# Masking the local attention on VectorE instead of by matmul, in an eight-stage transformer on one Trainium2 core

## The chip, the cores and the metric

The program runs on one core of a Trainium2 chip. The metric is the time of one launch in device microseconds. Before the change it is 4281.75 us, the median of 3 runs (4274.94 to 4282.47).

## What is computed

The reference chains eight stages over x of shape (2, 1024, 256). The change lies in one of them, the stage of `_L2_ffn_setup`: six layers, each a local attention followed by a gated feed-forward part.

```python
def attn_layer(x, Wqkv, qs, ksc, Wo):          # 16 heads of 64
    q, k, v = split(x @ Wqkv)
    q, k = l2norm(q) * qs, l2norm(k) * ksc     # l2norm: t / max(norm(t), 1e-12)
    q, k = rotary(q), rotary(k)
    # windows of 64 rows; each looks at the window before it and at itself: 128 keys
    sim = einsum(q, [k before, k own]) * 8
    sim = where(key later than the row, or over 64 before it, or absent, -max, sim)
    return softmax(sim) @ [v before, v own] -> @ Wo

def ffn_layer(x, g, bln, W1, b1, W2, b2):      # inner width 682
    a, gate = split((layernorm(x) * g + bln) @ W1 + b1)
    return (a * gelu(gate)) @ W2 + b2
```

Both are residual: each is added to x. A token shift precedes the projections.

## The kernel before

All work is written out by hand: each engine has its own list of instructions, in the order in which it executes them, and the engines meet by semaphores. A layer is two blocks, one for attention and one for the feed-forward part; at the end of a block the engines wait for each other.

**Attention** (lines 1660 to 1985). The 2048 tokens are 16 tiles of 128 rows, and each tile has two halves of 8 heads, so a layer has 32 halves, u = 2n + i. The engines work on different halves at once:

- TensorE (PE), for each u: `turn_ready(u)` (L1715, transposes of q and k), `project(n+1, i, 0)` and `project(n+1, i, 1)` (L1705: q and k of the half two ahead), `scores(u)` (L1742, L1747), `turn_probs(u-1)` (L1715), `project(n+1, i, 2)` (v), `attend(u-1)` (L1764). In the last tile `attention_out` (L1776), 16 matmul records, stands in the place of the projections. A projection writes PSUM bank 0 or 1 in turn, and waits until the bank's last contents are read: part 0 for `rotate` of the half before, part 1 for ScalarE's copy `value` of the half before, part 2 for `rotate` of part 0.
- ScalarE (ACT), for each u: `turned_query` (L1831), `turned_key` (L1838, L1839), `value` (L1859), `norms` (L1822, L1824), `square` twice (L1814), `turned_probs(u-1)` twice (L1845), `exp(u)` (L1849), `out(u-1)` (L1864). ACT does them in this order; `out(u-1)` and all that follows stand behind `exp(u)`.
- VectorE (DVE), for each u: `rotate(n+1, i, 0)` (L1907, L1909), `shift(u)` (L1925 maximum, L1929 subtraction), `rotate(n+1, i, 1)`, `row_sums(u)` (L1936, L1938), `sums(n+1, i)` (L1917 twice, and the guard L1920, which takes the maximum with 1e-24).
- GpSimd (POOL), for each u: `scale_probs(u-1)` twice (L1985), `scale` twice (L1978, waits for `norms`), `pair` twice (L1972, each waits for its `rotate`).
- SyncE issues the copies of v into the next window's place (L1684, L1688).

The mask is a bf16 tile of 0 and -1e30, and `scores` first multiplies an identity by it into the PSUM bank (four matmuls of 64x64 by 512, L1742) and then adds the scores of q and k to it (16 matmuls, L1747). A fp32 matmul leaves two records in the trace. The next half's scores may start when `shift` has read the bank.

**Feed-forward part** (lines 2000 to 2250). It goes over four groups g of 512 tokens: `up` (L2090, L2095), GELU on ACT, `gated` on DVE (L2208), `down` (L2108), `add_ffn` on DVE (L2222). The inner width 682 makes five chunks of 128 rows and a rest of 42. `down(g)` goes for each of the two output halves c through the six chunks, the rest last, into PSUM bank c. TensorE's order ends with up(2), down(1), up(3), down(2), down(3).

## Time and profile before

| | |
|---|---|
| median of 3 runs | 4281.75 us (4274.94 to 4282.47) |
| the profiled execution | 4293.74 us, its span 4291.9 us |
| busy, share of the span | PE 91%, PEld (weight loads) 49%, DVE 58%, ACT 46%, POOL 38% |
| granted TensorE clock, mean | 0.958 |
| local transformer, six layers | from about 860 to 3877 us of the span; attention some 334 us of a layer, feed-forward some 169 |
| DMA | 43 GB/s mean over the span |

A row of a timeline has the start in us from the span's start, the time it took in us, the engine, the line of the kernel, the operation, the tile written <- tiles read, shapes, and how many instructions the row merges. In brackets behind it stands how long the engine was idle before it, and what it was waiting for.

### The profile page before, as it was taken

Reading aid. Unit: us, or ns where it says so; the run is one execution under the profiler, and the core shown is the slowest. Engines: PE = TensorE matmul, PEld = TensorE weight load, DVE = VectorE, ACT = ScalarE, POOL = GpSimd, SP = SyncE. Lnnn points to the kernel's source line nnn. Section 1 sums busy time; section 2 is a strip of 40 time slices with the busy share of each in tenths; the row PEclk is TensorE's granted clock in tenths of the full one; section 3 lists DMA queues with packets and bytes.
Section 4 is the critical chain, followed back from the end, with each engine's and each line's share of the span. In section 5 each row is a group of like instructions: output and inputs, shape, how many; then the busy total and the mean of one; then the engine's idle time right before and its main releaser. Section 6 shows DMA issues by size and latency. Waiting matters only on the chain. (4 is left out here: it accounts for less than half of the span.)

```text
span 4291.9 us, 68832 instructions
## 1 busy us (share of the span) xinstructions
PE 3893.8 (91%) x26876; PEld 2084.4 (49%) x26887; DVE 2490.1 (58%) x3426; ACT 1953.7 (46%) x3526; POOL 1637.2 (38%) x1428
## 2 busy tenths in 40 slices
PE   6769976899999999999999999999999999998755
PEld 4434333555544555445544555445554455545522
DVE  4564555578823886258842788238862588424533
ACT  3555443556622664336632566326643366323411
POOL 0520321066611664036630566116641366300044
PEclk9989987999999999999999999999999999998877
DMA  4010000111110111001110111101110011100296
GB/s 147 1 39 3 0 0 10 57 44 30 26 61 16 29 29 58 20 24 29 30 67 0 34 28 27 61 15 29 29 52 26 24 28 30 48 0 11 90 287 188
DMA packets 95344, 185.48 MB, mean 43 GB/s; under 512 B 14004, under 2 KB 46256, under 8 KB 94000
## 3 DMA queue, kind: packets, MB, share of 16 engines
q1 hardware_dynamic: 86816, 169.02, 13.2%
q0 software_dynamic: 6144, 9.44, 1.2%
q8 instruction: 217, 3.56, 0.4%
q10 hardware_dynamic: 2064, 2.62, 0.2%
q14 instruction: 103, 0.84, 0.1%
HBM read 112.19 MB, written 20.09 MB: 31 GB/s over the span
## 5 line engine op out<-in xcount | busy, mean ns | idle before, releaser
L1705 PE MATMUL PS<-locw,X 128*128 128x512 f32 x2304 | 1066.3, 599 | 28.9 <-PEq L133 13.1
L1972 POOL TENSOR_TENSOR locm<-locm 128x512 f32<-128x512 f32 x384 | 489.1, 1274 | 921.1 <-DVE locm L1909 920.8
L1705 PEld LDWEIGHTS PS<-locw,X 128*128 128x128 f32 x2304 | 394.9, 190 | 441.6 <-issue 309.8
L2090 PE MATMUL PS<-locxn,locw 128*128 128x512 f32 x960 | 435.9, 612 | 19.8 <-DVE loch L2208 19.8
L1978 POOL TENSOR_TENSOR locm<-locm,locrn 128x512 f32<-128x512 f32 x384 | 392.4, 1043 | 128.6 <-ACT locrn L1824 128.6
L1985 POOL TENSOR_TENSOR locpr<-locpr,locrs 128x512 f32<-128x512 f32 x384 | 391.0, 1039 | 128.8 <-DVE locrs L1938 109.0
L1907 DVE TENSOR_TENSOR locm<-PS,loctab 128x512 f32<-128x512 f32 x384 | 263.3, 686 | 211.8 <-ACT locsq L1814 211.8
L1845 ACT ACTIVATE locpt<-PS 128x512 f32<-128x512 f32 x384 | 208.4, 594 | 322.2 <-PE PS L1715 322.2
L2208 DVE SCALAR_TENSOR_TENSOR loch<-PS,locvec,locgl 128x512 f32<-128x512 f32 x144 | 106.8, 748 | 370.4 <-PE PS L2090 280.9
L2090 PEld LDWEIGHTS PS<-locxn,locw 128*128 128x128 f32 x960 | 185.9, 196 | 267.0 <-issue 237.2
L1849 ACT ACTIVATE locpr<-locpr 128x1024 f32<-128x1024 f32 x192 | 203.4, 1060 | 190.9 <-DVE locpr L1929 190.9
L1925 DVE TENSOR_REDUCE locnm<-PS 128x8 f32<-128x1024 f32 x192 | 234.8, 1223 | 87.0 <-PE PS L1747 81.9
L2108 PE MATMUL PS<-loch,locw 128*128 128x512 f32 (+1 forms) x576 | 265.4, 606 | 0.0
L1909 DVE TENSOR_TENSOR locm<-PS,loctab 128x512 f32<-128x512 f32 x384 | 261.1, 680 | 0.0
L1814 ACT ACTIVATE locsq<-PS 128x512 f32<-128x512 f32 x384 | 223.6, 589 | 42.9 <-PE PS L1705 27.9
L1929 DVE TENSOR_TENSOR locpr<-PS,locnm 128x1024 f32<-128x1024 f32 x192 | 235.1, 1224 | 6.6
L1936 DVE TENSOR_REDUCE locrs<-locpr 128x8 f32<-128x1024 f32 x192 | 234.2, 1220 | 6.7 <-ACT locpr L1849 6.7
L1917 DVE TENSOR_REDUCE locss<-locsq 128x8 f32<-128x512 f32 x384 | 238.0, 662 | 0.0
L2160 ACT ACTIVATE locgl<-PS,locvec 128x512 f32<-128x512 f32 x120 | 81.1, 686 | 343.3 <-PE PS L2090 343.1
L1764 PEld LDWEIGHTS PS<-locpt,locve 128*64 128x64 f32 x3072 | 154.9, 137 | 149.5 <-issue 132.0
L2069 PE MATMUL PS<-BIG,locwo 128*128 128x512 f32 x480 | 211.1, 597 | 5.7 <-PEq L1675 5.7
L1764 PE MATMUL PS<-locpt,locve 128*64 128x64 f32 x3072 | 198.8, 228 | 13.3 <-ACT locpt L1845 13.3
(326 smaller groups left out, 6363.4 us busy)
## 6 DMA issues: line engine op xcount, KB each, us to landing
locve<-locva SPq DMA_DIRECT2D x372, 128.0 KB, 2.2
locw<-in_L2f_wqkv SPq DMA_DIRECT2D x36, 512.0 KB, 9.9
BIG<-in_L3f_gu SPq DMA_DIRECT2D x16, 768.0 KB, 10.1
moe_sums<-none SPq DMA_DIRECT2D x2, 4352.0 KB, 24.0
locw<-in_L2f_w SPq DMA_DIRECT2D x6, 1386.0 KB
BIG<-moe_sums SPq DMA_DIRECT2D x16, 512.0 KB, 10.5
moewp<-in_L3f_gu SPq DMA_DIRECT2D x10, 768.0 KB, 14.4
loctab<-in_L2f_tabs SPq DMA_DIRECT2D x6, 1024.0 KB, 12.2
```

Of the source, the lines that this page charges most:

```text
L1705: mm = pe.matmul(PS[:, o % 2, :], k.X[:, j, at - j:at - j + P], W[:, j, col:col + G], start=j == 0, stop=j == KD - 1)
L1764: mm = pe.matmul(PS[r * HD:(r + 1) * HD, 6 + u % 2, t * P + w * WIN:t * P + (w + 1) * WIN], v[:, 8 * i + 2 * t + r, :], PT[:, 2 * (u % 2) ...
L1907: dve.tensor_tensor(heads(M1[:, j, :]), raw, tab[0], ALU.mult)
L1909: dve.tensor_tensor(M2[:, x, :].rearrange("p (h u d) -> p h u d", h=8, u=2), halves, tab[1].rearrange("p h (u d) -> p h u d", u=2), ALU.mu ...
L1917: op = dve.tensor_reduce(SS[:, i, m, :], heads(SQ[:, m, :]), AX.X, ALU.add)
L1925: dve.tensor_reduce(NM[:, u % 2, :], view, AX.X, ALU.max, negate=True).then_inc(s.negmax, 1)
L1929: dve.tensor_tensor(PR[:, u % 2, :, :], view, NM[:, u % 2, :].unsqueeze(2).to_broadcast([P, 8, P]), ALU.add).then_inc(s.shifted, 1)
L1972: pool.tensor_tensor(M1[:, j, :], M1[:, j, :], M2[:, x, :], ALU.add).then_inc(s.paired, 1)
L1978: pool.tensor_tensor(heads(M1[:, j, :]), heads(M1[:, j, :]), RN[:, i, x, :].unsqueeze(2).to_broadcast([P, 8, HD]), ALU.mult).then_inc(s.re ...
L1985: pool.tensor_tensor(pr, pr, RS[:, u % 2, 4 * x:4 * x + 4].unsqueeze(2).to_broadcast([P, 4, P]), ALU.mult).then_inc(s.probs, 1)
L2090: mm = pe.matmul(PS[:, 4 + 2 * (m % 2) + half, :], W1[:, c, at:at + P], XNL[:, g % 2, c, :], start=c == 0, stop=c == KD - 1)
L2108: mm = pe.matmul(PS[:, c, :], W2[0:r, m, c * P:(c + 1) * P], H[0:r, g % 2, m, :], start=m == 0, stop=m == FM - 1)
```

## The change

The mask no longer goes through TensorE. Its tile is fp32, 128 by 2 by 128 (a quarter of the size), and DVE adds it when it copies the scores from PSUM into the tile PR of the probabilities; the maximum and the subtraction then read PR. TensorE's wait before the next scores is for that first copy (`masked`). The rest is smaller: the guard of the sums takes its constant from a tile TINY by `tensor_tensor` instead of as an immediate by `tensor_scalar`; the squares of the two halves have buffers of their own, and ACT does the first square of a half ahead of `norms`; in `down` the rests of both output halves are laid on rows 0 to 41 and 64 to 105, with a second copy of the rest's weights (one more DMA) and of its activations (one more DVE copy for each group), and are multiplied after the ten full chunks; `down` alternates between banks 0, 1 and 2, 3.

```diff
-    mask = np.stack([np.tile(np.concatenate([v, own], 1), (1, 4)) for v in (none, before)], 1).astype(f)
+    earlier = [np.where(np.arange(P)[:, None] < WIN, none, before), before]
+    mask = np.stack([np.concatenate([v, own], 1) for v in earlier], 1).astype(f)
...
         def make_first(pool):
-            pool.wait_ge(s.mask_loaded, 16)
-            pool.tensor_copy(MASKB[:, :, :], MASKF)
             make_tables(pool, 0)
...
-                SQ = sa(f"locsq_{layer}", [P, 2, G])
+                SQ = sa(f"locsq_{layer}", [P, 2, 2, G])
...
                                 if u:
-                                    pe.wait_ge(s.shifted, HALVES * layer + u)
+                                    pe.wait_ge(s.masked, HALVES * layer + u)
...
                         def scores(u):
-                            for r in range(2):
-                                for w in range(2):
-                                    kind = 0 if n % NT == 0 and w == 0 else 1
-                                    pe.matmul(PS[w * WIN:(w + 1) * WIN, 4 + r, :], k.identb[...], MASKB[...], start=True, stop=False)
                             for t in range(4):
...
-                                                       start=False, stop=t == 3)
+                                                       start=True, stop=True)
...
                         def square(n, i, x):
-                            if n or i:
-                                act.wait_ge(s.sums_guarded, HALVES * layer + 2 * n + i)
-                            act.activation(SQ[:, x, :], PS[:, (3 * i + x) % 2, :], ACT.Square).then_inc(s.squared, 1)
+                            if n:
+                                act.wait_ge(s.sums_guarded, HALVES * layer + 2 * (n - 1) + i + 1)
+                            act.activation(SQ[:, i, x, :], PS[:, (3 * i + x) % 2, :], ACT.Square).then_inc(s.squared, 1)
...
                                 value((u - 1) // 2 + 1, (u - 1) % 2)
+                            if more:
+                                square(n + 1, i, 0)
+                            if u and (u - 1) // 2 < TILES - 1:
                                 norms((u - 1) // 2 + 1, (u - 1) % 2)
                             if more:
-                                square(n + 1, i, 0)
                                 square(n + 1, i, 1)
...
-                            dve.tensor_scalar(SS[:, i, :, :], SS[:, i, :, :], 1e-24, None, ALU.max).then_inc(s.sums_guarded, 1)
+                            dve.tensor_tensor(SS[:, i, :, :], SS[:, i, :, :], TINY[:, :, :], ALU.max).then_inc(s.sums_guarded, 1)
...
                         def shift(u):
-                            dve.wait_ge(s.scores, HALVES * layer + u + 1)
-                            dve.tensor_reduce(NM[:, u % 2, :], view, AX.X, ALU.max, negate=True).then_inc(s.negmax, 1)
-                            dve.wait_ge(s.negmax, HALVES * layer + u + 1)
                             if u >= 2:
                                 dve.wait_ge(s.turned_in_psum, probs_turn(u - 2, 1) + 1)
-                            dve.tensor_tensor(PR[:, u % 2, :, :], view, NM[:, u % 2, :].unsqueeze(2).to_broadcast([P, 8, P]),
+                            dve.wait_ge(s.scores, HALVES * layer + u + 1)
+                            dve.tensor_tensor(pr, view, MASK[:, kind, :].unsqueeze(1).to_broadcast([P, 8, P]),
+                                              ALU.add).then_inc(s.masked, 1)
+                            dve.wait_ge(s.masked, HALVES * layer + u + 1)
+                            dve.tensor_reduce(NM[:, u % 2, :], pr, AX.X, ALU.max, negate=True).then_inc(s.negmax, 1)
+                            dve.wait_ge(s.negmax, HALVES * layer + u + 1)
+                            dve.tensor_tensor(pr, pr, NM[:, u % 2, :].unsqueeze(2).to_broadcast([P, 8, P]),
                                               ALU.add).then_inc(s.shifted, 1)
...
                         def down(g):
                             pe.wait_ge(s.h, FM * (n0 + g) + FM + 2)
+                            pe.wait_ge(s.rest, n0 + g + 1)
+                            at = 2 * (g % 2)
                             for c in range(KD):
...
-                                for m in range(FM):
-                                    r = rows(m)
-                                    mm = pe.matmul(PS[:, c, :], W2[0:r, m, c * P:(c + 1) * P], H[0:r, g % 2, m, :],
-                                                   start=m == 0, stop=m == FM - 1)
-                                mm.then_inc(s.y_in_psum, 1)
+                                for m in range(FM - 1):
+                                    pe.matmul(PS[:, at + c, :], W2[0:FR, m, c * P:(c + 1) * P], H[0:FR, g % 2, m, :],
+                                              start=m == 0, stop=False)
+                            for c in range(KD):
+                                r = slice(c * GATE_AT, c * GATE_AT + last)
+                                pe.matmul(PS[:, at + c, :], W2[r, FM - 1, c * P:(c + 1) * P], H[r, g % 2, FM - 1, :],
+                                          start=False, stop=True).then_inc(s.y_in_psum, 1)
...
                         def gated(g):
...
+                            dve.wait_ge(s.h, FM * (n0 + g) + FM + 2)
+                            dve.tensor_copy(H[GATE_AT:GATE_AT + last, g % 2, FM - 1, :], H[0:last, g % 2, FM - 1, :]).then_inc(s.rest, 1)
```

## Rows read from the trace of the kernel before

**Rows 1.** Windows: busy us of PE, PEld, DVE, ACT, POOL, then clock; attention, feed-forward.

```profile
900.00:1000.00 100.00, 100.00 (x1006) 58.91 (x1005) 87.49 (x118) 63.00 (x127) 70.00 (x65) 1.00 0.13 30
1200.00:1340.00 140.00, 135.74 (x310) 57.84 (x306) 32.73 (x47) 40.67 (x54) 13.88 (x9) 0.98 0.13 46
```

**Rows 2.** Timeline of ACT: exp of one half, out and value behind it.

```profile
1011.88 1.06 ACT L1849 ACTIVATE locpr<-locpr 128x1024 f32<-128x1024 f32 x1 [0.89 <-DVE locpr L1929]
1013.15 0.60 ACT L1864 ACTIVATE BIG<-PS 128x512 f32<-128x512 f32 x1 [0.21 <-PE PS L1764]
...
1014.96 0.62 ACT L1859 ACTIVATE locva<-PS 128x512 f32<-128x512 f32 x1
```

**Rows 3.** Timeline of PE and PEld around two halves' scores.

```profile
1008.00 0.41 PE L1742 MATMUL PS<-locmaskb,identb 64*64 64x512 bf16 x4
1008.24 1.04 PE L1747 MATMUL PS<-lockt,locqt 64*64 64x128 f32 x32
...
1013.96 3.65 PE L1705 MATMUL PS<-locw,X 128*128 128x512 f32 x8
...
1015.63 0.30 PEld L1705 LDWEIGHTS PS<-locw,X 128*128 128x128 f32 x2 [0.61 <-ACT locva L1859]
```

**Rows 4.** Source L1859, who waited for it; source L1864, until when idle (us, times).

```profile
  PEld PS L1705: 106.5, 174
...
  PE PS L1764: 40.9, 160
```

**Rows 5.** Timeline of DVE in the same half.

```profile
1009.36 1.22 DVE L1925 TENSOR_REDUCE locnm<-PS 128x8 f32<-128x1024 f32 x1
1010.62 1.22 DVE L1929 TENSOR_TENSOR locpr<-PS,locnm 128x1024 f32<-128x1024 f32 x1
...
1015.61 0.96 DVE L1920 TENSOR_SCALAR locss<-locss 128x16 f32<-128x16 f32 x1
1017.58 0.69 DVE L1907 TENSOR_TENSOR locm<-PS,loctab 128x512 f32<-128x512 f32 x1 [1.01 <-ACT locsq L1814]
```

**Rows 6.** Timeline of POOL in the same half.

```profile
1009.66 1.27 POOL L1972 TENSOR_TENSOR locm<-locm 128x512 f32<-128x512 f32 x1
...
1014.50 2.04 POOL L1985 TENSOR_TENSOR locpr<-locpr,locrs 128x512 f32<-128x512 f32 x2
1017.21 1.04 POOL L1978 TENSOR_TENSOR locm<-locm,locrn 128x512 f32<-128x512 f32 x1 [0.67 <-ACT locrn L1824]
```

**Rows 7.** Sources: DVE operations by line, shortest/median/longest ns, first and last start.

```profile
L1929 DVE TENSOR_TENSOR locpr<-PS,locnm x192: 1223/1224/1226, 887.0 to 3696.7; 128x1024 f32<-128x1024 f32 x192
L1936 DVE TENSOR_REDUCE locrs<-locpr x192: 1219/1220/1222, 889.4 to 3699.0; 128x8 f32<-128x1024 f32 x192
L2559 DVE TENSOR_TENSOR moeroom<-moeroom,moets x1: 1225/1225/1225, 4072.2 to 4072.2; 128x1024 f32<-128x1024 f32 x1
L185 DVE TENSOR_TENSOR X<-lnxc,lnrs x8: 676/678/1607, 852.3 to 857.4; 128x512 f32<-128x512 f32 x8
L1920 DVE TENSOR_SCALAR locss<-locss x192: 174/957/959, 875.4 to 3676.7; 128x16 f32<-128x16 f32 x192
```

**Rows 8.** Timeline of ACT: exp of halves 0 and 29 of the first layer.

```profile
888.28 1.06 ACT L1849 ACTIVATE locpr<-locpr 128x1024 f32<-128x1024 f32 x1 [3.17 <-DVE locpr L1929]
...
1164.72 1.06 ACT L1849 ACTIVATE locpr<-locpr 128x1024 f32<-128x1024 f32 x1 [0.88 <-DVE locpr L1929]
```

**Rows 9.** Timelines of PE and DVE at the end of the first layer's feed-forward part.

```profile
1328.36 17.43 PE L2090 MATMUL PS<-locxn,locw 128*128 128x512 f32 x40
1345.63 1.88 PE L2095 MATMUL PS<-locxn,locw 128*106 128x512 f32 x4
...
1363.97 0.75 DVE L2222 SCALAR_TENSOR_TENSOR X<-PS,locvec,X 128x512 f32<-128x512 f32 x1 [4.79 <-PE PS L2108]
1369.51 0.75 DVE L2222 SCALAR_TENSOR_TENSOR X<-PS,locvec,X 128x512 f32<-128x512 f32 x1 [4.79 <-PE PS L2108]
```

**Rows 10.** Timeline of POOL: the tables made before the first layer.

```profile
861.77 4.49 POOL L1614 TENSOR_TENSOR loctab<-loctab,locrows 128x2048 f32<-128x2048 f32 x1 [8.41 <-DMA locrows<-in_L2f_rows]
```

More of the change, by code:

```diff
@@ L1568, in stage_local_transformer @@
     (
-        s.mask_loaded, s.weights, s.tables, s.tables_made, s.layer_vectors, s.wo_loaded, s.ffn_loaded, s.cleared,
+        s.mask_loaded, s.tiny, s.weights, s.tables, s.tables_made, s.layer_vectors, s.wo_loaded, s.ffn_loaded, s.cleared,
         s.projected, s.squared, s.rotated, s.paired, s.sums, s.sums_guarded, s.logs, s.norms, s.ready,
-        s.turned_in_psum, s.turned, s.scores, s.negmax, s.shifted, s.probs, s.values,
+        s.turned_in_psum, s.turned, s.scores, s.masked, s.negmax, s.shifted, s.probs, s.values,
         s.attended, s.recip, s.out, s.exps, s.rows_summed,
         s.wo_in_psum, s.x1, s.gate_in_psum, s.a_in_psum, s.gelu, s.h, s.y_in_psum, s.x2, s.mean_in_psum, s.xsum, s.centred, s.fsquared, s.sqsum,
-        s.var_in_psum, s.log_var, s.rstd, s.xnormed, s.affine
+        s.var_in_psum, s.log_var, s.rstd, s.xnormed, s.affine, s.rest
     ) = (sem("loc_" + n) for n in (
-        "mask_loaded", "weights", "tables", "tables_made", "layer_vectors", "wo_loaded", "ffn_loaded", "cleared",
+        "mask_loaded", "tiny", "weights", "tables", "tables_made", "layer_vectors", "wo_loaded", "ffn_loaded", "cleared",
         "projected", "squared", "rotated", "paired", "sums", "sums_guarded", "logs", "norms", "ready",
-        "turned_in_psum", "turned", "scores", "negmax", "shifted", "probs", "values",
+        "turned_in_psum", "turned", "scores", "masked", "negmax", "shifted", "probs", "values",
         "attended", "recip", "out", "exps", "rows_summed",
         "wo_in_psum", "x1", "gate_in_psum", "a_in_psum", "gelu", "h", "y_in_psum", "x2", "mean_in_psum", "xsum", "centred", "fsquared", "sqsum",
-        "var_in_psum", "log_var", "rstd", "xnormed", "affine"
+        "var_in_psum", "log_var", "rstd", "xnormed", "affine", "rest"
     ))
@@ L1594, in stage_local_transformer @@
         ROWS = sb("locrows", [P, 4 * HD])
-        MASKF = k.BIG[:, KD * T:KD * T + 2 * G].rearrange("p (u n) -> p u n", u=2)
-        MASKB = sb("locmaskb", [P, 2, G], BF16)
+        MASK = sb("locmask", [P, 2, P])
         VEC = sb("locvec", [P, 2 * KD + 2 * FM + KD])
@@ L1600, in stage_local_transformer @@
         WO = sb("locwo", [P, CH, D])
+        TINY = sb("loctiny", [P, 2, 8])
         W = sb("locw", [P, KD, WC])
@@ L1620, in load_first @@
             sp.dma_start(kept, Xf).then_inc(kept_saved, 16)
-            sp.dma_start(MASKF, io["L2f_mask"]).then_inc(s.mask_loaded, 16)
+            sp.dma_start(MASK[:, :, :], io["L2f_mask"]).then_inc(s.mask_loaded, 16)
             load_layer(sp, 0)
         def make_first(pool):
-            pool.wait_ge(s.mask_loaded, 16)
-            pool.tensor_copy(MASKB[:, :, :], MASKF)
             make_tables(pool, 0)
@@ L1633, in may_write @@
                 dve.sem_inc(q, 2)
+            dve.memset(TINY[:, :, :], 1e-24).then_inc(s.tiny, 1)
             dve.wait_ge(kept_saved, 16)
@@ L1738, in scores @@
                             n, i = divmod(u, 2)
-                            for r in range(2):
-                                for w in range(2):
-                                    kind = 0 if n % NT == 0 and w == 0 else 1
-                                    pe.matmul(PS[w * WIN:(w + 1) * WIN, 4 + r, :], k.identb[r * HD:(r + 1) * HD, r * HD:(r + 1) * HD],
-                                              MASKB[r * HD:(r + 1) * HD, kind, :], start=True, stop=False)
                             for t in range(4):
@@ L1947, in _ @@
                         dve.wait_ge(s.tables_made, layer + 1)
+                        if layer == 0:
+                            dve.wait_ge(s.mask_loaded, 16)
+                        dve.wait_ge(s.tiny, 1)
                         for i in range(2):
@@ L2031, in _ @@
                         sp.dma_start(W2[0:FR, 0:FM - 1, :], io["L2f_w2"][layer:layer + 1, 0:(FM - 1) * FR, :].rearrange("a (c p) n -> p (a c) n", p=FR)).then_inc(s.ffn_loaded, 16)
-                        sp.dma_start(W2[0:last, FM - 1, :], io["L2f_w2"][layer:layer + 1, (FM - 1) * FR:FI, :].rearrange("a p n -> p (a n)")).then_inc(s.ffn_loaded, 16)
+                        for at in (0, GATE_AT):
+                            sp.dma_start(W2[at:at + last, FM - 1, :], io["L2f_w2"][layer:layer + 1, (FM - 1) * FR:FI, :].rearrange("a p n -> p (a n)")).then_inc(s.ffn_loaded, 16)
                         if layer < DEPTH - 1:
@@ L2119, in _ @@
                         mean(2)
-                        pe.wait_ge(s.ffn_loaded, 48 * layer + 48)
+                        pe.wait_ge(s.ffn_loaded, 64 * layer + 64)
                         up(0)
@@ L2221, in add_ffn @@
                                 dve.wait_ge(s.y_in_psum, KD * (n0 + g) + c + 1)
-                                dve.scalar_tensor_tensor(out=x, in0=PS[:, c, :], scalar=b2[:, c:c + 1], in1=x,
+                                dve.scalar_tensor_tensor(out=x, in0=PS[:, 2 * (g % 2) + c, :], scalar=b2[:, c:c + 1], in1=x,
                                                          op0=ALU.add, op1=ALU.add).then_inc(s.x2, 1)
```

8 lines of the change are left out of this document (6 added, 2 removed).

## The prediction

> **What bounds the kernel now.** I read the table by stage first. In the attention TensorE counts as busy all the time and at the full clock of 2.4 GHz, DVE 87% of it, POOL 70%; in the feed-forward part TensorE alone is near its limit and DVE is at a quarter [rows 1]. So taking work from TensorE and giving it to DVE looks nearly free in both. But a busy TensorE only says that its queue was never empty. So I read one half of the attention next, engine by engine, and look for the chain that closes on itself. A half takes 9.55 us (the guard's successor starts at 1017.58, in the half before at 1008.03, and so does every other row).
>
> TensorE is packed, yet its weight load for the k projection sits idle 0.61 us until ScalarE's copy `value` of the last v has freed the bank [rows 3]; that wait comes in 174 of the 192 halves [rows 4]. So ScalarE's queue paces TensorE, by a hair. That queue has an order: exp of half u, then `out`, two copies of q and k, `value` [rows 2]. In front of `out` it idles only 0.21 us, for TensorE's `attend`, in 160 halves [rows 2, 4]. And exp waits for DVE's subtraction, which waits for the maximum, which waits for TensorE's scores [rows 2, 5]. This closes a ring: scores(u), maximum, subtraction, exp(u), out(u-1), copies, `value`, k projection, scores(u+1). The ring has 9.55 us less the idle time in front of `out`. An ACT instruction starts some 0.02 before the one ahead of it ends, so I take 0.23 of slack: the ring needs 9.32 of the 9.55.
>
> **The change part by part: the attention.** (1) The mask's four matmuls go: from their start to that of the scores 0.24 us [rows 3]. They lie in the ring and in TensorE's queue: 0.24 off both. (2) Where the ring had two DVE steps it has three: add, maximum, subtraction. Each waits for the one ahead, so a step costs its start-to-start time, 1010.62 - 1009.36 = 1.26 us [rows 5]. The new add reads PSUM and one tile, as the old subtraction did (1224 ns); the maximum on SBUF is like the row sums (1220 ns); the subtraction on two SBUF tiles like the one of the last stage (1225 ns) [rows 7]. So nothing gets cheaper by reading the copy, and the ring gets one step of 1.26 longer (bounds 1.20 to 1.30). (3) The ring: 9.32 - 0.24 + 1.26 = 10.34 us. TensorE's own work, 9.55 - 0.24 = 9.31 at most, fits inside, and so does DVE's: its half was 9.55 with 1.01 idle [rows 5]; 9.55 - 1.01 + 1.26 = 9.80, and less if the guard gets shorter.
>
> The new wait on DVE, between add and maximum, holds up the second `rotate` and the row sums, which is in the 9.80; the wait for the probabilities of two halves ago moves ahead of the add and was met a half before. So the half goes from 9.55 to 10.34 us. What the change loosens doesn't lie in the ring. That TensorE may start the next scores after the copy instead of after the subtraction: that wait is met long before, since the ring brings the next k projection no sooner. That ACT squares ahead of `norms`: it takes away DVE's idle 1.01 us before `rotate` [rows 5], but then DVE stands waiting for the scores instead. The square itself now stands ahead of `norms` in ACT's queue, behind `value`, where no engine of the ring waits for it.
>
> The guard: 0.96 us in a half, but 0.17 where POOL is idle [rows 5, 7]; it ends 0.03 after POOL's two scalings of the probabilities (1014.50 + 2.04, against 1015.61 + 0.96) [rows 5, 6]. So it waits for POOL. Its replacement reads two SBUF tiles, and a DVE operation of two SBUF tiles took 1607 ns instead of 678 in the one case where it met POOL [rows 7]. The new guard is therefore bounded by 0.17 and 0.96, and I take 0.96. Neither is in the ring: DVE's 9.80 holds the guard at 0.96. The Trainium skill (SBUF — State Buffer, SBUF: two separate sides) states the same of operations with two SBUF inputs against a GpSimd operation that reads SBUF: one of them waits for the whole of the other. By it this part of the change brings nothing.
>
> How many halves: exp(0) to exp(29) are 1164.72 - 888.28 = 276.44 us in the first layer [rows 8]; behind them stands the last tile, which TensorE paces with `attention_out` and which I leave as it is (it loses some 0.2 and gains as much). After: 29 x 10.34 = 299.9, less 0.5 for the first half, which has no `out`: 299.4. That is +22.9 us for a layer, +137 for six.
>
> **The feed-forward part.** TensorE paces it, so each record saved counts. A record of a full chunk takes (1345.63 - 1328.36) / 40 = 0.432 us. One half c of `down` has 12 records and takes 1369.51 - 1363.97 = 5.54, so 0.36 more than 12 x 0.432 = 5.18: the price of going to 42 rows and back [rows 9]. Now 20 full records come first, then the two rests on separate rows and in separate banks. The scores' 32 records of 128 columns would take 32 x 0.432 / 4 = 3.5 us one by one, and take 1.04 [rows 3]: matmuls on separate quarters of the array do run side by side. Together the rests take two records' time: 22 x 0.432 + 0.36 = 9.86 instead of 11.08, 1.22 saved for a group. If they don't, 24 x 0.432 + 0.36 = 10.73, 0.35 saved. I take 1.22. On the other side, both halves of the last `add_ffn` now come after the last matmul, where the first was hidden: 0.7 (one is 0.75 [rows 9]). A layer: 4 x 1.22 - 0.7 = 4.2, six: -25 us. The DVE copy of the activations and its wait stand behind the last `gated` operation of a group, with DVE idle 4.79 us before each addition [rows 9]; what is queued behind it (the next normalisation or addition) waits for ACT or TensorE anyway. I cost it at nothing; without that cover it would be some 0.5. TensorE's new wait for that copy stands at the head of `down`, with all of TensorE's queue behind it; the copy follows the group's last `gated` at once, and TensorE is then still in the next `up` or the last `down`. The extra DMA is issued at the block's start, ahead of the next layer's weights on SyncE, a whole feed-forward part before they are used.
>
> **The start.** The mask's DMA shrinks to a quarter. It is ahead of the tables in the queue, and the first layer waits for these (POOL idle 8.41 until they land) [rows 10]: 0 to -2, I take -1. The dropped copy on POOL stood in that idle time.
>
> **The sum.** 137 - 25 - 1 = +111 us. The profiled execution took 4293.74 (span 4291.9), so it would be 4405; it stood 12 above the median of the runs, 4281.75, which gives 4393.
>
> **The rivals.** A, the packing doesn't do what it says: the rests run one after the other, 0.87 x 4 x 6 = 21 us of the 25 are lost: 4414. For it: the rests are 128 columns wide, and the scores only 64. Against: separate rows and banks, as there.
>
> B, the port: the subtraction now reads two SBUF tiles, in the middle of the ring, and POOL is busy 70% [rows 1]. If POOL is at work when it starts, it waits for the rest of that instruction, as in the row of 1607 ns [rows 7]. Where does it start? Count from the end of the last subtraction (1011.84 before). POOL's scale starts 5.37 after it (1017.21) and two take 2.04, the pair behind them 1.27 [rows 6]: POOL is free from 8.68. The subtraction starts at 10.34 - 1.22 = 9.12, so 0.44 clear of it. It decides from there: if POOL gets 0.44 later, the wait grows up to 1.27. At half of that, 0.64 x 29 x 6 = 111: 4504. The same page of the Trainium skill makes this its rule; no row shows such a subtraction beside POOL.
>
> C, the other side: the ring isn't tight, because ScalarE has more room in front of `out` than the 0.21 shown (it decides from 1.02). Then TensorE's queue paces, and the half takes 9.31: 29 x 9.31 = 270.0, 6.4 saved for a layer, 38 for six, and with the 26 of the rest the time is 4218. For it: DVE and TensorE both have room on the table by stage, and DVE's idle 1.01 goes. Against: 174 waits of 192 for `value` [rows 4].
>
> D, in between: part of the add is hidden, and what is left is what the feed-forward part saves (0.15 us a half): no change, 4282.
>
> **How the numbers follow.** The forecast has 0.73, A 0.09, B 0.07, C 0.08, D 0.03. A measurement here can tell some 0.2% from no change, 9 us. The predicted time is 4393. Its own bounds: the step 1.20 to 1.30 is 10 us either way, the slack 0.2 to 0.3 as much, the feed-forward part -25 to -4, the start 2. So 4360 to 4425; C and most of B are left out, 0.15 of the chances. I widen it downwards a little for a ring that is not tight in all halves: 4350 to 4430. Faster: 0.08; the same: 0.03; slower: 0.89.
>
> **What would show it.** The distance of two exps in the attention at 10.3 us; the wait of the weight load for `value` as before; in front of `out` no idle time for `attend` left; DVE idle before the add, for the scores, by half a microsecond; the subtraction at 1225 ns and no longer; the guard at 0.96 or 0.17 with no effect; the k projection's weight load now truly holding up TensorE. In the feed-forward part the additions of both halves back to back, 9.9 after the last group's. Wrong would be: exps 9.3 apart (C), a subtraction well over 1.3 us (B), 10.7 between the groups of `down` (A).

## The result, and the profile after

The kernel after takes 4391.89 us (median of 4 runs, 4389.62 to 4392.59) against 4282.11 of the kernel before beside it: a ratio of 1.0252, 95% interval 1.0235 to 1.0269. The prediction was 4393. The profiled execution took 4389.62 us, its span 4387.8. Runs in the chip's slower state are left out of all medians here.

First the table by stage: a stretch of attention in the first layer, the columns as in [rows 1]. TensorE is no longer busy all the time, DVE has gone from 87% to 93%, and neither is full.

```profile
900.00:1000.00 100.00, 96.11 (x916) 55.10 (x916) 92.53 (x116) 57.30 (x116) 63.25 (x58) 1.00 0.12 26
```

One half in the timeline of ScalarE, DVE, TensorE and GpSimd, the same half for which [rows 2, 3, 5, 6] stand. (L1742 is now the scores, L1705 a projection, L1926, L1929 and L1931 add, maximum and subtraction, L1844 exp, L1859 `out`, L1854 `value`, L1917 the guard, L1977 `pair`.)

```profile
1008.30 1.07 ACT L1844 ACTIVATE locpr<-locpr 128x1024 f32<-128x1024 f32 x1 [2.20 <-DVE locpr L1931]
1009.27 0.58 ACT L1859 ACTIVATE BIG<-PS 128x512 f32<-128x512 f32 x1
1010.96 0.62 ACT L1854 ACTIVATE locva<-PS 128x512 f32<-128x512 f32 x1
1011.63 0.30 PEld L1705 LDWEIGHTS PS<-locw,X 128*128 128x128 f32 x2 [0.95 <-ACT locva L1854]
1012.05 0.96 DVE L1917 TENSOR_TENSOR locss<-locss,loctiny 128x16 f32<-128x16 f32 x1
1013.55 1.10 PE L1742 MATMUL PS<-lockt,locqt 64*64 64x128 f32 x32
1014.79 1.23 DVE L1926 TENSOR_TENSOR locpr<-PS,locmask 128x1024 f32<-128x1024 f32 x1 [0.58 <-PE PS L1742]
1015.64 1.28 POOL L1977 TENSOR_TENSOR locm<-locm 128x512 f32<-128x512 f32 x1
1016.05 1.22 DVE L1929 TENSOR_REDUCE locnm<-locpr 128x8 f32<-128x1024 f32 x1
1017.30 1.22 DVE L1931 TENSOR_TENSOR locpr<-locpr,locnm 128x1024 f32<-128x1024 f32 x1
1018.56 1.07 ACT L1844 ACTIVATE locpr<-locpr 128x1024 f32<-128x1024 f32 x1 [2.20 <-DVE locpr L1931]
```

The ring can be read round: scores at 1013.55, three DVE steps, exp at 1018.56, and in the half before exp at 1008.30, `out` at once behind it (no idle time left), the copies, `value`, then the weight load for the k projection that had waited 0.95 us for `value`, and the scores. Exp to exp is 10.26 us. DVE idles 0.58 for the scores. The subtraction starts 0.38 us after `pair` ends (1015.64 + 1.28 against 1017.30) and takes 1.22.

The last group of the feed-forward part, for [rows 9]:

```profile
1369.94 8.75 PE L2117 MATMUL PS<-loch,locw 128*128 128x512 f32 x20
1378.61 1.13 PE L2121 MATMUL PS<-loch,locw 42*128 42x512 f32 x4
1379.78 1.41 DVE L2236 SCALAR_TENSOR_TENSOR X<-PS,locvec,X 128x512 f32<-128x512 f32 x2 [7.72 <-PE PS L2121]
1389.61 1.41 DVE L2236 SCALAR_TENSOR_TENSOR X<-PS,locvec,X 128x512 f32<-128x512 f32 x2 [8.43 <-PE PS L2121]
```

The four records of the rests take 1.13 us, additions come in pairs, and a group is 9.83 us (1389.61 - 1379.78) where it was 11.08.

Where the 95.9 us between the two spans lie, rounded, by the starts of the exps, of the additions and of the layers in both timelines, six layers together: start of a layer to the first exp +6; first to second exp +12; the next 28 halves +121 (0.72 each on average); the last tile +1.5, and -1.7 from there to VectorE's second residual addition in the feed-forward part's block; the rest of the feed-forward part -37; all other stages -7, which the change doesn't touch. The profiled execution before stood 12 above its median, so that the medians differ by more, 110.

### The profile page after: what moved, and what is told of

Its sections match the earlier page's. It is cut to its first block and busy times, and to the rows that moved or that the text cites. A ratio compares the mean times of both kernels' runs of the same rounds, so it can differ in the third digit from the quotient of the medians.

```text
span 4387.8 us, 67521 instructions
## 1 busy us (share of the span) xinstructions
PE 3908.3 (89%) x26119; PEld 2065.0 (47%) x26119; DVE 2720.2 (62%) x3643; ACT 1933.4 (44%) x3526; POOL 1637.0 (37%) x1427
## 5 line engine op out<-in xcount | busy, mean ns | idle before, releaser
L1705 PE MATMUL PS<-locw,X 128*128 128x512 f32 x2304 | 1128.2, 615 | 107.0 <-DVE locm L1906 64.3
L1977 POOL TENSOR_TENSOR locm<-locm 128x512 f32<-128x512 f32 x384 | 488.7, 1273 | 1027.1 <-DVE locm L1906 1026.6
L1705 PEld LDWEIGHTS PS<-locw,X 128*128 128x128 f32 x2304 | 397.7, 191 | 600.5 <-issue 320.3
L2096 PE MATMUL PS<-locxn,locw 128*128 128x512 f32 x960 | 424.8, 600 | 19.9 <-DVE loch L2220 19.9
L1844 ACT ACTIVATE locpr<-locpr 128x1024 f32<-128x1024 f32 x192 | 204.3, 1064 | 434.1 <-DVE locpr L1931 434.1
L1926 DVE TENSOR_TENSOR locpr<-PS,locmask 128x1024 f32<-128x1024 f32 x192 | 235.1, 1225 | 173.5 <-PE PS L1742 173.5
L1809 ACT ACTIVATE locsq<-PS 128x512 f32<-128x512 f32 x384 | 229.3, 597 | 70.9 <-PE PS L1705 68.8
L1906 DVE TENSOR_TENSOR locm<-PS,loctab 128x512 f32<-128x512 f32 x384 | 260.3, 678 | 0.0
L1931 DVE TENSOR_TENSOR locpr<-locpr,locnm 128x1024 f32<-128x1024 f32 x192 | 235.1, 1224 | 6.6
L1929 DVE TENSOR_REDUCE locnm<-locpr 128x8 f32<-128x1024 f32 x192 | 234.2, 1220 | 6.6
L1742 PEld LDWEIGHTS PS<-lockt,locqt 64*64 64x64 f32 x6144 | 165.5, 132 | 145.6 <-issue 145.6
```

Source lines behind the costliest of these rows:

```text
L1705: mm = pe.matmul(PS[:, o % 2, :], k.X[:, j, at - j:at - j + P], W[:, j, col:col + G], start=j == 0, stop=j == KD - 1)
L1906: dve.tensor_tensor(M2[:, x, :].rearrange("p (h u d) -> p h u d", h=8, u=2), halves, tab[1].rearrange("p h (u d) -> p h u d", u=2), ALU.mu ...
L1926: dve.tensor_tensor(pr, view, MASK[:, kind, :].unsqueeze(1).to_broadcast([P, 8, P]), ALU.add).then_inc(s.masked, 1)
L1929: dve.tensor_reduce(NM[:, u % 2, :], pr, AX.X, ALU.max, negate=True).then_inc(s.negmax, 1)
L1931: dve.tensor_tensor(pr, pr, NM[:, u % 2, :].unsqueeze(2).to_broadcast([P, 8, P]), ALU.add).then_inc(s.shifted, 1)
L1977: pool.tensor_tensor(M1[:, j, :], M1[:, j, :], M2[:, x, :], ALU.add).then_inc(s.paired, 1)
```

## The experiments

The theory is the ring of the prediction, with three DVE steps in it. The rivals: DVE's queue as a whole, the port that DVE and GpSimd share, and the smaller edits (guard, order of the squares). "Half" is the distance of two exps in the middle of a layer; the ratio is to runs of the kernel before beside each. e12 leaves out part of the computation.

| kernel | half, us | first half | median, us | ratio to before (95%) |
|---|---|---|---|---|
| before | 9.55 | 9.42 | 4282.11 | |
| after | 10.26 | 11.49 | 4391.89 | 1.0252 (1.0235 to 1.0269) |
| e1_value_first | 9.87 | 11.49 | 4327.62 | 1.0108 (1.0090 to 1.0126) |
| e2_mask_on_pe | 9.55 | 8.73 | 4255.78 | 0.9922 (0.9891 to 0.9952) |
| e3_mask_alone | 10.68 | 10.7 to 11.5 | 4505.97 | 1.0524 (1.0505 to 1.0543) |
| e4_pool_extra | 11.07 | 11.8 | 4537.92 | 1.0606 (1.0579 to 1.0633) |
| e5_square_back | 10.68 | 11.49 | 4484.74 | 1.0480 (1.0457 to 1.0503) |
| e6_no_guard | 10.26 | 11.49 | 4393.00 | 1.0266 (1.0240 to 1.0291) |
| e7_loose | 10.25 | 10.25 | 4382.43 | 1.0247 (1.0218 to 1.0276) |
| e8_loose_mask_on_pe | 9.50 | 8.52 | 4237.36 | 0.9912 (0.9892 to 0.9933) |
| e9_loose_out_late | 10.25 | 10.25 | 4372.03 | 1.0214 (1.0192 to 1.0236) |
| e10_rests_one_by_one | 10.26 | 11.4 | 4428.34 | 1.0349 (1.0331 to 1.0368) |
| e11_sums_first | 10.25 | 10.25 | 4379.69 | 1.0230 (1.0199 to 1.0261) |
| e12_short_pair | 9.47 | 9.29 | 4245.32 | 0.9929 (0.9908 to 0.9949) |

**e1: `value` taken out of the ring.**

```diff
                             turned_key(u)
-                            if u and (u - 1) // 2 < TILES - 1:
-                                value((u - 1) // 2 + 1, (u - 1) % 2)
...
+                            if more:
+                                value(n + 1, i)
                             exp(u)
```

> The kernel after, with ScalarE's copy `value` of a half placed ahead of the exp of the same half instead of behind the next half's copies of q and k. The v projection ends at 1007.07 and the exp starts at 1008.30 in the trace of after, so the copy fits in ScalarE's idle 2.20 us. Ring theory: the three DVE steps no longer stand between two scores; what is late next is DVE's own queue (10.26 less the 0.59 it idles before the add = 9.67 us) or the second rotate with both projections behind it (10.26 less TensorE's 0.63 of waiting for `value` = 9.63). So a half takes 9.6 to 9.75 instead of 10.26, and the time is 4391 - 0.6 x 29 x 6 = about 4287 (4275 to 4300). Rival 1, the three DVE steps cost their time by themselves (DVE's queue bounds at 10.26): a half stays 10.26 and the time 4391. Rival 2, TensorE's queue bounds as soon as ScalarE is out of the way: 9.31, 4391 - 0.95 x 29 x 6 = 4226.

Moving a copy of 0.62 us that costs about the same in either place (0.60 here) took 0.39 us off the half and 64 off the time. So the three steps cost because they stand in a ring with `value`; DVE's queue is not what binds at 10.26. But the half stopped at 9.87, above the expected 9.6 to 9.75. Timeline of TensorE and DVE (L1906 ends the second rotate):

```profile
1007.46 3.70 PE L1705 MATMUL PS<-locw,X 128*128 128x512 f32 x8 [0.28 <-DVE locm L1906]
1011.09 1.10 PE L1742 MATMUL PS<-lockt,locqt 64*64 64x128 f32 x32
1012.33 1.23 DVE L1926 TENSOR_TENSOR locpr<-PS,locmask 128x1024 f32<-128x1024 f32 x1 [0.20 <-PE PS L1742]
```

Next in line, as the rows show, is a ring of its own: second rotate, q and k projections (3.63), scores (1.24 to the add), add, maximum, subtraction, rotate. DVE still idles 0.20, so its queue is at 9.67 as expected, but not what binds. I had taken off all 0.63 us of TensorE's waiting; what `value` had delayed, from the q projection to the scores, is 4.03 (1009.52 to 1013.55 in after) less 3.63 = 0.40.

**e2 and e3: the mask part alone, undone and done.** e2 is after with the mask's four matmuls, its bf16 tile and the old `shift` put back; e3 is before with `shift`, the fp32 tile and the wait on `masked` of after. The hunks are those of the diff above.

> The kernel after with the mask part alone undone: four mask matmuls on TensorE, maximum and subtraction on PSUM; the feed-forward packing, the two-tile guard, the square buffers and ScalarE's new order stay. Ring theory: the half is back at 9.55 (9.5 to 9.6) and the first half back by 2 us, so 4391 - 0.71 x 29 x 6 - 2 x 6 = 4255 (4240 to 4265), and the feed-forward part keeps its 6 us a layer. Rival, the loss comes from the guard or from the order of squares and norms: the half stays near 10.26 and the time near 4391.

> The kernel before with the mask part alone: DVE adds the mask on its copy of the scores, takes the maximum and subtracts from there; guard, squares, norms and feed-forward part stay as before. Ring theory: a half takes 10.26 and the time is 4282 + 0.71 x 29 x 6 + 2 x 6 = 4418 (4405 to 4435). The feed-forward part takes the 169 us of before; if its gain of 2 us a layer by the clock in after was chance, it may show some of that too (up to -12). Rival, the new order of square and norms is part of the loss: 4300 to 4380.

e2 came out as expected: the mask part is the whole loss, and what is left of the change is a gain of 0.8% on before. e3 did not: 10.68 and 4506. DVE in e3 (L1900 first rotate, L1922 add):

```profile
1015.37 0.69 DVE L1900 TENSOR_TENSOR locm<-PS,loctab 128x512 f32<-128x512 f32 x1 [1.01 <-ACT locsq L1807]
...
1016.58 1.22 DVE L1922 TENSOR_TENSOR locpr<-PS,locmask 128x1024 f32<-128x1024 f32 x1
```

DVE waits 1.01 us for a square ahead of the first rotate, and nothing ahead of the add: the scores no longer hold it up.

**e5: only the order of the squares undone; e6: no guard.**

```diff
-                            if more:
-                                square(n + 1, i, 0)
                             if u and (u - 1) // 2 < TILES - 1:
                                 norms((u - 1) // 2 + 1, (u - 1) % 2)
                             if more:
+                                square(n + 1, i, 0)
                                 square(n + 1, i, 1)
```

```diff
-                            act.activation(rn, ss, ACT.Ln, scale=LOG_SCALE).then_inc(s.logs, 1)
+                            act.activation(rn, ss, ACT.Ln, scale=LOG_SCALE, bias=TINY[:, 0, 0:1]).then_inc(s.logs, 1)
...
-                            op.then_inc(s.sums, 1)
-                            dve.wait_ge(s.sums, HALVES * layer + 2 * n + i + 1)
-                            dve.tensor_tensor(SS[:, i, :, :], SS[:, i, :, :], TINY[:, :, :], ALU.max).then_inc(s.sums_guarded, 1)
+                            op.then_inc(s.sums_guarded, 1)
```

> The kernel after with one line of its change undone: ScalarE does both squares of a half behind `norms` again, as before. Theory: with the mask on DVE a second ring is close to the first (guard, norms, squares, first rotate, add, maximum, subtraction, exp, row sums, GpSimd's scaling of the probabilities, guard), and the first square ahead of norms is what opens it. Then a half takes 10.68 as with the mask part alone, DVE idles 1.0 us before the first rotate and nothing before the add, and the time is 4391 + 0.42 x 28 x 6 = 4462 (4450 to 4475). Rival, the prediction's reading that this order lies in no ring: the half stays 10.26 and the time 4391, and the difference between the mask part alone and the whole change is due to the guard or the square buffers.

> The kernel after without DVE's guard: the constant 1e-24 goes into the logarithm of norms as its bias, on ScalarE, and DVE is rid of the 0.96 us. By the prediction the guard lies in no ring that binds: the half stays 10.26, DVE idles 0.59 + 0.96 = 1.55 before the add, and the time stays 4391 (4380 to 4400). Rival, DVE's queue or the way over norms binds: the half falls by up to 0.4, to 4320.

e5 has the 10.68 of e3 and the same idle 1.01 ahead of the first rotate; so the one line of order is worth 0.42 us a half, some 70 us, once the mask is on DVE. (Its time is 22 us above the expectation; the half is as expected, and most of the rest are the clock steps of the last section.) e6 is after without the guard, where that ring is open: the guard is worth nothing measurable there, 10.26 again. Whether taking out the guard would open the ring of e5 as well, no run shows; its guard ends 0.03 us after GpSimd's scalings there (1006.42 + 0.96 against 1005.31 + 2.04), as in [rows 5, 6].

**e4: one more GpSimd instruction ahead of `pair`.**

```diff
                             if n < TILES - 1:
+                                if u:
+                                    pool.tensor_tensor(EXTRA[:, :], TAB[:, 0:2, :].rearrange("p a b -> p (a b)"),
+                                                       TAB[:, 2:4, :].rearrange("p a b -> p (a b)"), ALU.add).then_inc(s.extra, 1)
+                                    pool.wait_ge(s.extra, (2 * TILES - 3) * layer + u)
                                 for x in range(2):
                                     pair(n + 1, i, x)
```

> The kernel after with one more GpSimd instruction in each half, an addition of two table slices into a tile that nobody reads (128x512, some 1.27 us), ahead of the first `pair`. In after the first `pair` ends at 1016.92 and the subtraction starts at 1017.30. If a DVE instruction on two SBUF tiles waits for a whole GpSimd instruction that is under way: `pair` now ends at 1018.2, the subtraction that would start at 1017.30 takes 2.1 to 2.2 us instead of 1.22, a half takes 10.26 + 0.95 = 11.2 and the time is 4391 + 0.95 x 29 x 6 = 4556 (4530 to 4580). If not: GpSimd has room (5.9 of 10.26 busy), the half stays 10.26, the subtraction 1.22 and the time 4391.

DVE's subtraction and GpSimd in e4:

```profile
1013.54 1.28 POOL L2009 TENSOR_TENSOR locextra<-loctab 128x512 f32<-128x512 f32 x1
1014.90 1.27 POOL L1978 TENSOR_TENSOR locm<-locm 128x512 f32<-128x512 f32 x1
...
1015.21 2.05 DVE L1932 TENSOR_TENSOR locpr<-locpr,locnm 128x1024 f32<-128x1024 f32 x1
```

`pair` ends at 1016.17, the subtraction 1.09 later, and it took 2.05 instead of 1.22. The half grew by 0.81. Rival B is real; in after it stayed away by 0.38 us.

**e7, e9, e11, e12: both rings opened, and a third.** e7 has `value` as in e1, no guard as in e6, and

```diff
-                            shift(u)
                             if more:
                                 rotate(n + 1, i, 1)
-                            elif i:
+                            shift(u)
+                            if not more and i:
```

> The mask on DVE as in after, with both rings opened: `value` ahead of the exp of its own half, the second `rotate` ahead of the add (so that the q projection of the next half doesn't wait behind add, maximum and subtraction), and no guard on DVE, since with it the second square would stand behind it. DVE's queue is then 9.67 - 0.96 = 8.7 and TensorE's is the longest: 9.87 less 0.28 of idle time and 0.16 of slower weight loads behind it, 9.4 to 9.45. Time 4391 - 0.84 x 28 x 6 - 6 x 1.5 = 4241 (4225 to 4260), below before. Rival, the subtraction now meets GpSimd's `pair`: 1.25 becomes up to 2.5 and the half 9.9 or more, 4320.

The half stayed at 10.25. The subtraction takes 1.70 now, and TensorE waits 0.70 for the copy of k, which stands behind `out`. I took that wait for what binds and put `out(u - 2)` behind `turned_key(u)`:

> The opened order with the mask on DVE (half 10.25, where TensorE waits 0.70 us for ScalarE's copy of k ahead of the last matmuls of the k projection, and the subtraction takes 1.69 us beside GpSimd's `pair`), with ScalarE's `out` of a half placed behind the next half's copies of q and k. If the ring is now scores, add, maximum, subtraction, exp, out, copies of q and k, scores, it loses the 0.47 us from the start of `out` to that of the copy of q: the half is 9.75 to 9.8 and the time 4382 - 0.47 x 28 x 6 = 4303 (4290 to 4315). If `out` is not in it, or another wait takes its place at once (TensorE for the scaled probabilities), the half stays within 0.1 of 10.25 and the time near 4382.

Again 10.25, with the same wait of 0.70. DVE's queue was full but for 1.12 us ahead of the row sums, so I filled that gap, `sums(n + 1, i)` ahead of `row_sums(u)`:

> The opened order with `out` behind the copies (half 10.25), with DVE's `sums` of the next tile ahead of the row sums. `out` turned out not to be in the ring, and TensorE's 0.70 us of waiting for the copy of k not what bounds. New theory: DVE's queue itself binds, add, maximum, subtraction, then 1.12 us of idle time for the exp, row sums, sums, both rotates; `sums` (1.24) doesn't need the exp and fills that gap, so DVE's half falls by some 1.0 to 1.1, to 9.1 to 9.2, and TensorE's queue binds at 9.4 to 9.5: 4372 - 0.8 x 28 x 6 = 4238 (4225 to 4260). If DVE's queue doesn't bind, the half stays 10.25 and the time 4372; if GpSimd now meets the subtraction longer, 9.6 to 10 and 4270 to 4340.

10.25 a third time. DVE got that gap filled, but now idles 0.77 ahead of the first rotate, and the subtraction takes 2.00 instead of 1.71. Timeline of e11 (L1989 scaling of the probabilities, L1982 scaling, L1976 `pair`, L1930 subtraction, L1937 and L1939 row sums and reciprocal):

```profile
1003.24 2.04 POOL L1989 TENSOR_TENSOR locpr<-locpr,locrs 128x512 f32<-128x512 f32 x2 [3.74 <-DVE locrs L1939]
1005.24 2.04 POOL L1982 TENSOR_TENSOR locm<-locm,locrn 128x512 f32<-128x512 f32 x2
1007.24 2.51 POOL L1976 TENSOR_TENSOR locm<-locm 128x512 f32<-128x512 f32 x2
1008.83 2.00 DVE L1930 TENSOR_TENSOR locpr<-locpr,locnm 128x1024 f32<-128x1024 f32 x1
1010.86 1.06 ACT L1844 ACTIVATE locpr<-locpr 128x1024 f32<-128x1024 f32 x1 [2.29 <-DVE locpr L1930]
1011.95 1.22 DVE L1937 TENSOR_REDUCE locrs<-locpr 128x8 f32<-128x1024 f32 x1
1013.20 0.20 DVE L1939 RECIPROCAL locrs<-locrs 128x8 f32<-128x8 f32 x1
1013.49 2.04 POOL L1989 TENSOR_TENSOR locpr<-locpr,locrs 128x512 f32<-128x512 f32 x2 [3.74 <-DVE locrs L1939]
```

GpSimd works without a gap from 1003.24 to 1009.75, the subtraction ends 1.08 after that, then exp, row sums, reciprocal, and GpSimd starts again at 1013.49: 10.25 round. One link of this ring is no semaphore but the port. In e7 and e9 too the subtraction ends 1.08 after `pair`.

> Leaves out part of the computation: GpSimd's second `pair` of a half adds 64 of the 512 columns only, so the rotation of k is incomplete; all else as in the opened order with `sums` first (half 10.25, subtraction 2.00 us). Last theory, a ring without a semaphore: GpSimd runs scaling of the probabilities, scaling and `pair` back to back (2.00 + 2.00 + 2.51), the subtraction waits for the last `pair` and ends 1.08 behind it, then exp 1.1, row sums and reciprocal 1.3, hand-over 0.25, and GpSimd starts again: 10.25 in all three opened kernels. With the second `pair` about 1.0 us shorter the subtraction takes 1.22 again and the ring falls to 9.2, below TensorE's queue: half 9.4 to 9.5, time 4380 - 0.8 x 28 x 6 = 4246 (4230 to 4265). If the ring runs over DVE's queue or ScalarE's copies alone, the subtraction gets shorter, but the half stays at 10.0 or more and the time above 4340.

```diff
+                            to = G if x == 0 else HD
-                            pool.tensor_tensor(M1[:, j, :], M1[:, j, :], M2[:, x, :], ALU.add).then_inc(s.paired, 1)
+                            pool.tensor_tensor(M1[:, j, 0:to], M1[:, j, 0:to], M2[:, x, 0:to], ALU.add).then_inc(s.paired, 1)
```

```profile
1006.10 1.55 POOL L1977 TENSOR_TENSOR locm<-locm 128x512 f32<-128x512 f32 x2
1007.69 1.22 DVE L1930 TENSOR_TENSOR locpr<-locpr,locnm 128x1024 f32<-128x1024 f32 x1
```

With `pair` 0.96 us shorter, the subtraction starts behind its end and takes 1.22, and the half falls by 0.78 to 9.47: the port ring is shown. (What sets 9.47 is not TensorE's queue, as expected, but a further ring; see e8.) The Trainium skill (SBUF — State Buffer, SBUF: two separate sides) states the rule, that a DVE operation on two SBUF inputs and a GpSimd one that reads SBUF exclude each other for a whole instruction. These runs agree for a DVE operation that meets a GpSimd one under way: it ends 1.08 to 1.09 us after that one (e4, e7, e9, e11). They also show that this wait can close a ring.

**e8: the opened order with the mask on TensorE.** e2 with the edits of e7.

> The same opened order with the mask on TensorE (four mask matmuls, maximum and subtraction on PSUM). If TensorE's own work was what set the 9.55 of before (mask 0.24, scores 0.97, turns 0.93, v 1.81, attend 1.08, turns 0.93, q and k 3.58: sum 9.54), nothing is gained: 9.55 a half and 4256, so that the mask on DVE is the better one by 0.1 to 0.15 a half, 17 to 25 us. If the wait for `value` was what set it, the half falls to 9.3 to 9.4 and the time to about 4225.

It has the shortest time of all here that compute the whole, 0.9912 of before; to e2, 0.9922, the intervals overlap. TensorE, then PEld, DVE, ACT and POOL, in a stretch of one half of e8 with the mask's matmuls, and of e12 without:

```profile
1003.00:1012.48 9.48, 9.48 (x98) 5.74 (x97) 7.49 (x11) 5.97 (x12) 6.48 (x7) 1.00 0.13 29
```

```profile
1002.95:1012.42 9.47, 9.47 (x93) 5.56 (x92) 8.60 (x12) 5.86 (x12) 5.55 (x7) 1.00 0.13 28
```

TensorE counts as busy all the time in both, but only in e8 does its queue set the half. The timeline of e8 (L1707 projections, L1744 mask, both of TensorE), then that of e12 (L1705 projections, L1742 scores, L1844 exp, L1834 the end of the copy of k, L1809 square, L1905 first rotate, L1925 add):

```profile
1005.86 3.60 PE L1707 MATMUL PS<-locw,X 128*128 128x512 f32 x8
1009.39 0.41 PE L1744 MATMUL PS<-locmaskb,identb 64*64 64x512 bf16 x4
```

```profile
1008.74 3.75 PE L1705 MATMUL PS<-locw,X 128*128 128x512 f32 x8
1008.95 1.06 ACT L1844 ACTIVATE locpr<-locpr 128x1024 f32<-128x1024 f32 x1 [1.52 <-DVE locpr L1930]
1010.87 0.39 ACT L1834 ACTIVATE lockt<-PS 128x256 f32<-128x256 f32 x1
1011.37 0.30 PEld L1705 LDWEIGHTS PS<-locw,X 128*128 128x128 f32 x2 [0.71 <-issue]
1011.61 0.62 ACT L1809 ACTIVATE locsq<-PS 128x512 f32<-128x512 f32 x1
1012.26 0.69 DVE L1905 TENSOR_TENSOR locm<-PS,loctab 128x512 f32<-128x512 f32 x1 [0.76 <-ACT locsq L1809]
1012.42 1.10 PE L1742 MATMUL PS<-lockt,locqt 64*64 64x128 f32 x32
1014.66 1.22 DVE L1925 TENSOR_TENSOR locpr<-PS,locmask 128x1024 f32<-128x1024 f32 x1
1018.42 1.06 ACT L1844 ACTIVATE locpr<-locpr 128x1024 f32<-128x1024 f32 x1 [1.52 <-DVE locpr L1930]
```

In e8 the q and k projections hold TensorE for 3.53 us (1005.86 to 1009.39), with no wait in them, and the half is 9.50. In e12 they hold it for 3.68 (1008.74 to 1012.42): the weight load for their last two records starts 0.71 after the one ahead of it has ended, where the others have 0.24. The profile names no releaser for it, but it starts 0.11 after the copy of k ends, for which the program waits at that place (the same copy that it names in e9, with 0.70). So TensorE loses 0.15 in a half of e12, and its own work without the mask is 9.47 - 0.15 = 9.32. Taking the mask off TensorE's queue is worth 9.50 - 9.32 = 0.18 us a half, not 0.24: without the mask ahead of them the scores hold TensorE for 1.03 instead of 0.97.

What sets e12's 9.47 is a ring over ScalarE and DVE, with no TensorE in it: exp, the copies of q and k, `out`, the first square, both rotates, add, maximum, subtraction, exp. From 1008.95 to 1018.42 ScalarE and then DVE go through it without a gap. It is read from the trace; no run opens it.

**e10: the rests on the same rows.**

```diff
-                                r = slice(c * GATE_AT, c * GATE_AT + last)
+                                r = slice(0, last)
```

> The kernel after with the rests of both output halves on the same rows 0 to 41, still behind the ten full chunks and in their own banks; the second copy of the rest is made but not read. If separate rows are what lets the two run side by side (rival A the other way round): the four records take 4 x 0.432 + 0.36 = 2.1 instead of the 1.13 us that the trace of after shows, a group of `down` 10.5 to 10.7 instead of 9.83, and the time is 0.6 to 0.87 x 4 x 6 = 14 to 21 longer, 4405 to 4413. If separate banks suffice, the group stays at 9.83 and the time at 4391.

```profile
1378.36 1.61 DVE L2236 SCALAR_TENSOR_TENSOR X<-PS,locvec,X 128x512 f32<-128x512 f32 x2 [7.72 <-PE PS L2121]
1389.05 1.61 DVE L2236 SCALAR_TENSOR_TENSOR X<-PS,locvec,X 128x512 f32<-128x512 f32 x2 [9.08 <-PE PS L2121]
```

A group takes 10.69 us instead of 9.83, so it is the separate rows that let the rests run side by side. The time rose by 36 rather than 14 to 21. Of that 4 x 0.86 - 0.7 = 2.7 a layer, 16 for six, are the rests (the 0.7 is the first of the last two additions, which is hidden again); most of the other 20 are clock steps (last section).

## Why the prediction was right

**The ring** is shown (e1, e2), and its size was close: 10.26 for 10.34. The terms, from the rows of before and after. The third step: from the first DVE step to the exp 2.52 (9.36 to 11.88 [rows 2, 5]) became 3.77, +1.25 for 1.26. The slack on ScalarE, exp to `value`: 3.08 became 2.66, -0.42, where I had taken 0.23: besides the 0.21 of idle time ahead of `out`, the exp and `out` each give up their place some 0.10 sooner when `out` doesn't wait. The mask, end of `value` to the first DVE step: 3.33 became 3.21, -0.12, where I had 0.24. 9.55 + 1.25 - 0.42 - 0.12 = 10.26. Two mis-sized terms, -0.19 and +0.12, cancel in part; that is luck. In before the wait for `value` itself held TensorE up by only 0.05 of a half (the q and k projections 3.58 us against e8's 3.53), so "by a hair" was right.

**TensorE's own work, "9.31 at most"**, held within 0.01 us: 9.32 (e12, less its wait). Part of that is luck, since the mask is worth 0.18 and not 0.24, and 9.55 contained the 0.05. So rival C had TensorE's price right. But no kernel here reaches it: with the ring open, other rings close at 9.87 (e1), 10.25 (e7, e9, e11) and 9.47 (e12).

**The first half.** I took 9.8 for it; it is 11.49, 10 us for six layers. TensorE waits for the second rotate, which now stands behind three DVE steps, and then works at 0.72 of the clock. First the wait, then the window (columns as in [rows 1]):

```profile
895.44 4.96 PE L1705 MATMUL PS<-locw,X 128*128 128x512 f32 x7 [2.27 <-DVE locm L1906]
```

```profile
895.00:901.00 6.00, 5.56 (x16) 2.25 (x20) 5.06 (x8) 3.06 (x9) 4.06 (x4) 0.72 0.10 22
```

In e7, with that rotate ahead of the add, the first half is 10.25. Ahead of it the first exp of a layer also comes 1.1 us later in most layers, by the new DVE step, which I had left out (in e2, without that step, it is gone).

**"What the change loosens doesn't lie in the ring"** was half right, and the price was missing. For the guard it holds (e6: 10.26). The wait of the scores was not tried alone; in the rows of after the add of one half ends at 1016.02 and the next scores start at 1023.81. The order of the squares was needed: without it the half is 10.68 (e3, e5), and the time 4485 or more. The rows of before had it: DVE idled 1.01 for the square ahead of the first rotate, and not at all ahead of the maximum [rows 5], so its own ring, guard, norms, squares, rotate, stood close to the other: within some 0.1 us, if the 10.68 of e3 less the step of 1.26 is its size before, 9.42. My 9.55 - 1.01 + 1.26 = 9.80 took that 1.01 as removable, and it is the moved square that removes it here.

**The guard** takes 957 ns in the median as before [rows 7]: the two tiles changed nothing, and I was right to take 0.96. But the 0.17 is not the guard beside an idle GpSimd: in before all 192 guards, the twelve of 0.17 too, end 0.03 to 0.05 us after a GpSimd instruction does.

**The feed-forward part.** The packing is worth 11.08 - 9.83 = 1.25 for a group (1.22 predicted), less the additions, 4 x 1.25 - 0.7 = 4.3 a layer, 26 for six (25 predicted). Measured are 37; the other 11 go with the clock, which falls there in every layer of before, and for fewer records and in every second layer only of after: windows around the group `up(1)` of before, layers one and three, and of after, layers one and two:

```profile
1272.00:1280.00 8.00, 7.27 (x13) 3.17 (x14) 2.09 (x3) 1.21 (x3) 2.23 (x1) 0.79 0.01 2
2273.00:2281.00 8.00, 7.02 (x10) 2.90 (x11) 1.65 (x3) 1.33 (x3) 2.47 (x1) 0.57 0.00 0
```

```profile
1299.00:1307.00 8.00, 7.49 (x18) 3.42 (x19) 2.18 (x4) 1.55 (x3) 2.00 (x1) 1.00 0.01 2
1817.00:1825.00 8.00, 7.43 (x14) 3.41 (x15) 1.93 (x3) 1.42 (x3) 2.07 (x1) 0.79 0.00 0
```

**The start.** The -1 can't be told from noise: the first projection starts at 866.6 us in before, at 871.5 in after, and anywhere from 860 to 872 in the other kernels.

**The rivals.** A: the rests do run together (e10 shows its case, 10.69 for my 10.73). B didn't occur: the subtraction took 1224 ns in all layers, its margin was 0.38 for my 0.44, and e4 shows the price just beyond. C and D fall with the half of 10.26. (D's 4282 lay outside the range too, so it left out 0.18 of the chances, not 0.15.)

**The sum.** Attention +141 for +137, packing -26 for -25; the clock's -11, the -1.7 ahead of the feed-forward part and the -7 in other stages were not foreseen, so that between the two profiled executions it was 96 and not 111. But the one of before stood 12 above its median and the one of after 2 below: the medians differ by 110. That the end is 1 us off is partly luck.

## What to carry to other kernels

When work moves to an engine with room to spare, ask whether it lands in a ring, and list every ring within the size of the step: here five, in one kernel or another, lay between 9.4 and 10.7 us. A wait that the trace shows need not be in the ring that binds; what shows the ring is a chain that returns to its own start with no gap, and an instruction that grows to the end of another engine's is a link of it. Nor does an engine that counts as busy all the time have to be what binds: TensorE did in e8 and in e12, and waited 0.15 us of each half in e12. Open the ring first and see which engine is then full: e8, with the order opened and the mask still on TensorE, has the shortest time here of those that compute the whole.

## What the runs showed of the hardware that was not expected

TensorE's clock goes in steps that look like noise of the kernel. From the exp of the last half of a layer to VectorE's second residual addition in the feed-forward part's block it is 18.6 us or 20.1 to 20.3 in nearly all layers of all kernels: after has 18.61 six times, e10 20.31 in five layers of six, though that stretch has the same code. In the long ones four records, following a short wait, stand 0.85 us apart instead of 0.43, 4 x 0.42 = 1.70 us, the lower of the clock's two levels, 1.2 GHz, instead of 2.4. The same stretch of the second layer in after and in e10, the granted clock third from the end:

```profile
1744.50:1754.50 10.00, 8.31 (x51) 4.25 (x50) 0.69 (x1) 1.61 (x3) 1.09 (x1) 1.00 0.57 199
```

```profile
1745.90:1755.90 10.00, 8.31 (x47) 4.05 (x46) 0.69 (x1) 1.60 (x3) 1.08 (x1) 0.83 0.59 204
```

Similar steps appear at the start of a layer and in `up(1)`. What decides whether the clock falls after such a wait stays open. Such steps add some 20 us to e5 and to e10, whose edits lie elsewhere, so that an effect of that size should be read from the stage, not from the sum.
